# A two layer gated cross attention kernel: layer 0 without mask rows, queries in three transfers, gelu in four parts, value projections at 7, 8 and 10, first loads in order of need on two queues

## What is computed

```python
def _L0_xattn_ref(query, key, value, Wq, bq, Wk, bk, Wv, bv, Wo, bo):   # query is _layernorm(x)
    q = split_heads(query @ Wq.T + bq)
    k = split_heads(key @ Wk.T + bk)
    v = split_heads(value @ Wv.T + bv)
    scores = jnp.einsum('bhqd,bhkd->bhqk', q, k) / np.sqrt(HEAD_DIM)
    weights = jax.nn.softmax(scores, axis=-1)
    out = jnp.einsum('bhqk,bhkd->bhqd', weights, v)
    return out.transpose(0, 2, 1, 3).reshape(b, -1, D_MODEL) @ Wo.T + bo
# layer 1: the same, with scores = jnp.where(m == 0, -1e9, scores) before the softmax
# layer 0's experts: D 128, F 512; layer 1's: D 128, H 64, and a shared one
h = jax.nn.gelu(jnp.einsum('td,edf->etf', xf, w1) + b1[:, None, :], approximate=False)
y = jnp.einsum('etf,efd->etd', h, w2) + b2[:, None, :]
```

## Time and profile before

| | us |
|---|---|
| median of 3 runs | 1044.85 (1041.06 to 1046.26) |
| the profiled execution | 1040.23 |
| its span, first to last instruction | 1038.1 |
| PE busy | 922.5 (89%) |
| DVE busy | 723.0 (70%) |
| ACT busy | 586.2 (56%) |
| POOL busy | 525.0 (51%) |

### The profile page before, as it was taken

How to read it: one execution, slowest core, us unless ns; L and a number is a source line. 1 busy time by engine, 2 the same in 40 slices (tenths; PEclk the granted TensorE clock), 3 DMA queues, 4 the chain that set the end, 5 groups by cost and what they waited for, 6 DMA issues and landing times.

```text
span 1038.1 us, 32346 instructions
## 1 busy us (share of the span) xinstructions
PE 922.5 (89%) x13088; PEld 675.9 (65%) x13088; DVE 723.0 (70%) x1531; ACT 586.2 (56%) x1060; POOL 525.0 (51%) x667
## 2 busy tenths in 40 slices
PE   2487899999999999999999999999999999999974
PEld 0154577777777777777777777666666666666753
DVE  3376576785767768586785867878787878787722
ACT  1044556556565565656547565665757575757560
POOL 5353445543546335453446565665657576672202
PEclk9998899999999999999999999999999999999995
DMA  8735653333323333233465646767676767665200
GB/s 181 133 90 137 145 126 72 72 83 69 63 55 85 70 77 76 37 81 70 95 137 88 143 110 132 162 123 156 124 152 122 145 130 146 137 137 97 52 2 18
DMA packets 95215, 107.24 MB, mean 103 GB/s; under 512 B 22394, under 2 KB 86972, under 8 KB 95068
## 3 DMA queue, kind: packets, MB, share of 16 engines
q1 hardware_dynamic: 95068, 105.19, 49.0%
HBM read 35.89 MB, written 0.46 MB: 35 GB/s over the span
## 4 chain that ended last, share of the span: by engine, by line
PE 66%; DVE 16%; ACT 9%; issue 5%; SPq 2%; DMA 1%; POOL 0%; POOLq 0%; ACTq 0%; DVEq 0%
PE pO L993 13%; PE pMX L1010 12%; PE pST L972 12%; PE pKV L1124 6%; PE pFY L1082 6%; PE pKV L1115 5%; PE pFH L1150 5%; DVE mx L925 4%; DVE mx L920 4%; ACT P L678 3%; DVE rden L839 3%; PE pFY L1047 2%; ACT HR L715 1%; PE pFY L1086 1%; ACT V L696 1%
## 5 line engine op out<-in xcount | busy, mean ns | idle before, releaser
L678 ACT ACTIVATE P<-pST 125x448 f32<-125x448 f32 x768 | 396.1, 542 | 349.9 <-PE pST L972 344.3
L925 DVE TENSOR_REDUCE mx<-pMX 112x1 f32<-112x500 f32 x384 | 258.4, 673 | 172.3 <-PE pMX L1010 172.1
L1010 PE MATMUL pMX<-kop,qmax 104*112 104x500 f16 x768 | 293.1, 392 | 44.7 <-DMA qmax<-qlo 18.5
L972 PE MATMUL pST<-qexp,kop 106*128 106x112 f16 (+1 forms) x3072 | 280.2, 214 | 19.9 <-ACT P L678 9.3
L972 PEld LDWEIGHTS pST<-qexp,kop 106*128 106x128 f16 (+1 forms) x3072 | 209.9, 102 | 127.1 <-issue 42.9
L920 DVE TENSOR_REDUCE mx<-pMX 112x1 f32<-112x500 f32 x384 | 255.8, 666 | 42.8 <-PE pMX L1010 41.9
L993 PE MATMUL pO<-P,V 125*17 125x112 f32 x6144 | 186.0, 262 | 0.0
L993 PEld LDWEIGHTS pO<-P,V 125*17 125x17 f32 x6144 | 136.8, 98 | 46.2 <-issue 36.3
L1010 PEld LDWEIGHTS pMX<-kop,qmax 104*112 104x112 f16 x768 | 99.0, 132 | 93.1 <-issue 21.7
L563 POOL CAST khi<-kfull 128x500 f16<-128x500 f32 x96 | 57.7, 601 | 193.0 <-ACT kfull L691 192.8
L565 POOL TENSOR_TENSOR klo<-kfull,khi 128x500 f16<-128x500 f32 x96 | 109.0, 1135 | 7.8
(11 more groups left out here) (144 smaller groups left out, 1089.6 us busy)
## 6 DMA issues: line engine op xcount, KB each, us to landing
C<-in_ctxT SPq DMA_DIRECT2D x32, 750.0 KB, 6.2
kop<-khi SPq DMA_DIRECT2D x192, 125.0 KB
kop<-maskop SPq DMA_DIRECT2D x48, 437.5 KB
kop<-klo SPq DMA_DIRECT2D x96, 125.0 KB
qexp<-qmax SPq DMA_DIRECT2D x32, 182.0 KB
maskin<-in_mask SPq DMA_DIRECT2D x8, 656.2 KB, 6.2
kop<-maskop SPq DMA_DIRECT2D x2, 1312.5 KB
qmax<-qhi SPq DMA_DIRECT2D x128, 7.0 KB
```

The source lines that it names most:

```text
L678: nc.scalar.activation(P[0:KP, slot, h * 4 * T:(h + 1) * 4 * T], pST[0:KP, h, 0:4 * T], ACT.Exp, scale=EXP_SCALE).then_inc(exp_done, 1)
L925: nc.vector.tensor_reduce(mx[:, s % 2, m // PAIRS, m % PAIRS:m % PAIRS + 1], pMX[0:T, 1, 0:CW], AX.X, ALU.max).then_inc(max_done, 1)
L972: mm = nc.tensor.matmul(pST[0:cols, h, i * T:(i + 1) * T], kop[0:ROWS, b, p, tile * KP:tile * KP + cols], qexp[0:ROWS, b, p, :, :].rearran ...
L1010: nc.tensor.matmul(pMX[0:T, m % 2, 0:CW], qmax[0:SHIFT0, st.s % 2, p, :, :].rearrange("r j q -> r (j q)"), kop[0:SHIFT0, st.s % 2, p, c * ...
```

## The change

- In layer 0 kop, qmax and qexp use 48 rows of keys or queries (`SHIFT0_L0`) and the two shift rows behind them (`ROWS_L0` = 50); no mask and pick rows. The two batches that open layer 1 get shift rows and pick rows by extra transfers. pick is now a 56 x 56 tile, repeated by the transfer.
- DVE writes the queries block-diagonally (head 0 of a pair with zeros beside it, head 1 likewise), multiplied by a column `head_of`; qmax is filled by three transfers per batch instead of six, and no longer cleared at the start.
- The largest scores in ct are laid out by halves of the pairs, and go to qexp in two transfers instead of one.
- Gelu of layer 0 is taken in four parts instead of two, two experts each; gelu stands at kt 9 instead of 8. `experts_of` lets y0 read the first part and y1 the second.
- In even steps with experts (`has_f`) the value projections stand at 7, 8, 10 instead of 8, 9, 10, and at kt 10 PE runs maxima, weighted sums and the projection ahead of the experts and both score halves behind them; ACT copies the values of kt 10 before the exponentials there.
- The first loads come in pieces in the order of need (weights of the keys, x of the first two batches, C in three chunks, the rest); the low halves of the first context and the weights are made by DVE in between. ACT's queue takes the biases, the queries of batch 0, the shift rows and the output weights.

The diff, cut to its core:

```diff
-        uses += [(8, "v0", 1), (9, "v1", 1), (10, "v2", 1)]
+        first = 7 if has_f(s) else 8
+        uses += [(first, "v0", 1), (first + 1, "v1", 1), (10, "v2", 1)]
...
-        uses += [(4, "qT", 2), (5 if s < 0 else 6, "q", 1)]
+        uses += [(2, "qT", 2), (3, "q", 2)] if s < 0 else [(4, "qT", 2), (6, "q", 2)]
...
+        pick = sb("pick", [S, S], F16)
+        shift_rows = sb("shift_rows", [2, SHW], F16)
...
+        def queries(eng, n):
+
+            for row, part in ((0, qhi), (PR, qhi), (2 * PR, qlo)):
+                eng.dma_start(qmax[row:row + PR, n % 2, :, :, :], part[:, n % 2, :, :]).then_inc(qmax_in, 16)
+            if opens_layer(n):
+                eng.dma_start(qmax[MASK0:SHIFT0, n % 2, :, :, :].rearrange("s p j q -> s (p j) q"),
+                              pick[:, :].unsqueeze(1).broadcast_to([S, H, S])).then_inc(qmax_in, 16)
...
-            sp.dma_start(W[:, :], wpack).then_inc(w_in, 16)
-            sp.dma_start(bq_row[:, :], bqrow).then_inc(w_in, 16)
-            sp.dma_start(bc[:, :], bcast.partition_broadcast(128)).then_inc(w_in, 16)
-            sp.dma_start(C[:, :], ctxT[0]).then_inc(c_in, 16)
-            sp.dma_start(X[:, :].rearrange("t (g d) -> t g d", g=G),
-                         x.rearrange("(g t) d -> t g d", g=G)).then_inc(x_in, 16)
-            sp.wait_ge(init_v, 1)
-            sp.wait_ge(init_p, 5)
-            for b in range(2):
-                sp.dma_start(kop[MASK0:SHIFT0, b, :, :],
-                             maskop[0:S, :].unsqueeze(1).broadcast_to([S, PAIRS, S2])).then_inc(init_dma, 16)
-                for i in range(2):
-                    sp.dma_start(kop[SHIFT0 + i:SHIFT0 + i + 1, b, :, :],
-                                 shift_rows[:, i:i + 1, :].broadcast_to([1, PAIRS, S2])).then_inc(init_dma, 16)
-                sp.dma_start(qmax[MASK0:SHIFT0, b, :, :, :],
-                             pick[:, :, :].rearrange("s (p j) q -> s p j q", j=2)).then_inc(init_dma, 16)
+            sp.dma_start(W[:, 0:D], wpack[:, 0:D]).then_inc(wk_in, 16)
+            sp.dma_start(xg(0), x[0:T, :]).then_inc(x0_in, 16)
+            for c in range(CH):
+                sp.dma_start(C[:, c * CW:(c + 1) * CW], ctxT[0, :, c * CW:(c + 1) * CW]).then_inc(c0_in[c], 16)
+            sp.dma_start(W[:, D:], wpack[:, D:]).then_inc(w_in, 16)
+            sp.dma_start(X[:, D:].rearrange("t (g d) -> t g d", g=G - 1),
+                         x[T:, :].rearrange("(g t) d -> t g d", g=G - 1)).then_inc(x_in, 16)
+            sp.dma_start(bc[:, :], bcast.partition_broadcast(128)).then_inc(bc_in, 16)
...
+                if opens_layer(n) and c == CH - 1:
+                    sp.dma_start(kop[SHIFT0:ROWS, dst, :, :].rearrange("r p (i n) -> r (p i) n", n=SHW),
+                                 shift_rows[:, :].unsqueeze(1).broadcast_to([2, PAIRS * S2 // SHW, SHW])
+                                 ).then_inc(kop_in[c], 16)
...
-                    sp.dma_start(qexp[SHIFT0:ROWS, (s - 1) % 2, :, :, :].rearrange("r p j q -> r (p j q)"),
-                                 ct[:, :]).then_inc(shift_in, 16)
+                    for h in range(2):
+                        row = SHIFT0_L0 if layer_of(s - 1) == 0 else SHIFT0
+                        to = qexp[row:row + 2, (s - 1) % 2, HP * h:HP * (h + 1), :, :]
+                        sp.dma_start(to.rearrange("r p j q -> r (p j q)"), ct[PAIRS * h:PAIRS * (h + 1), :]
+                                     ).then_inc(shift_in, 16)
...
+            def early_loads(s, kt):
+
+                if s == -1 and kt == 5:
+                    act.wait_ge(fh_free, upto(fh_uses, s, "q", True))
+                    queries(act, 0)
+                if s == 0 and kt == 0:
+                    act.wait_ge(init_p, 2)
+                    for b in range(2):
+                        act.dma_start(kop[SHIFT0_L0:ROWS_L0, b, :, :].rearrange("r p (i n) -> r (p i) n", n=SHW),
+                                      shift_rows[:, :].unsqueeze(1).broadcast_to([2, PAIRS * S2 // SHW, SHW])
+                                      ).then_inc(init_dma, 16)
+                if s == 0 and kt == 11:
+                    act.wait_ge(init_w, 4)
+                    for g in range(4):
+                        rows = slice(32 * g, 32 * g + PR)
+                        act.dma_start(woE[rows, :, :, :], wo.rearrange("l (r g i) n -> g i l r n", r=2, g=4)[g]
+                                      ).then_inc(wo_in, 16)
+                        act.dma_start(bvE[rows, :, :], bvc.rearrange("l g i r -> g i l r")[g]).then_inc(wo_in, 16)
+                    act.wait_ge(bc_in, 16)
+                    nc.scalar.activation(gains[:, :], bc[:, GX:GX + 4], ACT.Tanh).then_inc(init_a, 1)
...
+                for kt in range(KT):
+                    if has_f(s) and kt == 10:
+                        evacuate(kt)
...
-                    if kt == 8 and has_f(s):
+                    if kt == 9 and has_f(s):
                         act.wait_ge(fh_free, st.at(lambda s: before(fh_uses, s + 1, True)))
                         if layer_of(s - 3) == 0:
-                            for half in (HR[:, 0:E0 * F0C // 2, :], HR[:, E0 * F0C // 2:, :]):
-                                nc.scalar.activation(half, half, ACT.Gelu).then_inc(gelu_done, 1)
+                            for part in range(4):
+                                two = HR[:, 2 * F0C * part:2 * F0C * (part + 1), :]
+                                nc.scalar.activation(two, two, ACT.Gelu).then_inc(gelu_done, 1)
...
-                        link(nc.vector.tensor_copy(qhi[:, :], pFH[:, 0:T]))
-                        nc.vector.tensor_tensor(qlo[:, :], pFH[:, 0:T], qhi[:, :], ALU.subtract).then_inc(fh_free, 1)
+                            dve.wait_ge(qmax_in, q_total(s))
+                        if s == -1:
+                            dve.wait_ge(init_h, 7)
+                        q = pFH[:, 0:T].rearrange("p (b q) -> p b q", b=2)
+                        own = head_of[:, layer_of(s + 1), :]
+                        for j in range(2):
+                            link(nc.vector.tensor_scalar(qhi[:, :, j, :], q, own[:, j:j + 1], None, ALU.mult))
+                        for j in range(2):
+                            nc.vector.scalar_tensor_tensor(out=qlo[:, :, j, :], in0=q, scalar=own[:, j:j + 1],
+                                                           in1=qhi[:, :, j, :], op0=ALU.mult, op1=ALU.subtract
+                                                           ).then_inc(fh_free, 1)
...
+                    if s == -1 and kt == 1:
+                        low_context(0)
+                        query_weights()
+                        low_context(1)
+                    if s == -1 and kt == 2:
+                        low_context(2)
+                    if s == -1 and kt == 5:
+                        other_weights()
...
+                rows, slot = slice(0, SHIFT0_L0 if layer_of(n) == 0 else SHIFT0), i
+                nc.tensor.matmul(pMX[0:T, m % 2, 0:CW], qmax[rows, b, slot, :, :].rearrange("r j q -> r (j q)"),
+                                 kop[rows, b, slot, c * CW:(c + 1) * CW], start=True, stop=True).then_inc(mx_ready, 1)
...
+                    m0 = MAXES_PER_KT * kt
+                    apart_ = has_m(s)
                     late = kt in (1, 7)
-                    if has_m(s) and not late:
-                        max_scores(st, MAXES_PER_KT * kt)
-                    weigh(st, kt)
                     experts = [u[1] for u in fy_uses(s) if u[0] == kt and early(u[1])]
                     if experts:
+                        if has_m(s):
+                            max_scores(st, m0)
+                        weigh(st, kt)
+                        project(kt)
+                        if has_m(s):
+                            max_scores(st, m0 + 1)
                         small("y0")
-                        if has_m(s):
-                            max_scores(st, MAXES_PER_KT * kt + 1)
                         small("y1")
-                    score_half(st, kt, 0)
-                    if has_m(s) and late:
-                        max_scores(st, MAXES_PER_KT * kt)
...
-                    if has_m(s) and not experts:
-                        max_scores(st, MAXES_PER_KT * kt + 1)
-                    score_half(st, kt, 1)
+                        score_half(st, kt, 0)
+                        score_half(st, kt, 1)
```

More of the change, by code:

```diff
@@ L210, in pool_links, with opens_layer, b_total, q_total @@
     return n
[L213 to L215 removed]
+def opens_layer(n):
+    return n in (B, B + 1)
+def b_total(n, c):
+    return sum(48 if layer_of(t) == 0 else 80 if opens_layer(t) and c == CH - 1 else 64 for t in range(n + 1))
+def q_total(n):
+    return sum(48 if layer_of(t) == 0 else 64 if opens_layer(t) else 48 for t in range(n + 1))
+def qexp_total(n):
+    return 16 * (n // 2 + 1)
 class Step:
@@ L502, in step @@
                         apart(sp)
-                        sp.wait_ge(qexp_in[(s - 1) % 2], st.at(lambda s: 16 * ((s - 1) // 2 + 1)))
```

(8 more changed lines are left out.)

310 lines of the change are left out of this document (181 added, 129 removed).

## The result

The changed kernel takes 1078.49 us (median of 4 runs, 1075.65 to 1087.02) against 1045.22 for the kernel before: a ratio of 1.0335, 95% interval 1.0294 to 1.0376. It is 3.35% slower, where 1031.6 was forecast. The profiled execution has a span of 1077.8 us against 1038.1, so 39.7 us have to be found.

What follows compares the result with a forecast made beforehand. PE was taken as nearly full in the steps and nearly idle in a 38 us start. Terms -18.1 + 2 + 4.9 - 2 = -13.2, from the median 1044.85, gave 1031.6 us, range 1021 to 1040.

Steps and rivals of the forecast that it cites:

- No mask rows in layer 0: Layer 0's matmuls: time goes by columns, so fewer rows give PE 0; extra transfers opening layer 1 at most 3 us once.
- Rival 3: After the start: PE's clock stays low, running 18 us longer at half pace and losing 9 us: 1040.6; chance 8%.
- The start: First loads and queries: first maxima start at 20.0 instead of 38.11 us, -18.1 us.
- the forecast's far end: In the start: first maxima at 24.7 if queries land 5.2 us after the last issue's start and C's issue stalls.
- the rule on shared engines: In the start: transfers from different issuers share 16 DMA engines, so first maxima come up to 2.4 us after 20.0.
- The queries: Odd steps, DVE: four instructions instead of two, 0.22 us a step in layer 0, 0.42 in layer 1: +4.9 us.
- Gelu and value projections: Even steps: reordered work ends them 0.1 us earlier in layer 0, 0.15 in layer 1: -2 us (-20 to +10).
- The shift rows: Two transfers instead of one, second issue 0.6 us later where PE already waits: +2 us (0 to 5).
- Rival 1: Even steps around kt 9: the reorder removes most waits on ACT, up to -20 us instead of -2: 1023; chance 12%.
- rival 2: The start is cut less: first maxima at 24.7 instead of 20.0 us, total 1036; chance 18%.
- Rival 4: Even steps: PE stands through a table load and the four quarters' extra 0.4 us, +27 us: 1061; chance 4%.

Runs made afterwards that it cites:

- undivided: The changed kernel, with layer 0's matmuls on 48 and 50 rows issued with PE's array undivided: 1045.33 us (ratio 1.0030).
- the runs on 106, 66 and 50 rows: Changed kernel's early start, array undivided, old queries from batch 2 on, layer 0's maxima and scores on these rows: 1029.79, 1036.31, 1048.44 us.
- the zeros on 66 rows: An earlier run: the changed kernel, layer 0's maxima and scores on 66 rows, 16 of them zeros written by transfers: 1046.43 us (ratio 1.0013).
- the old queries: Changed kernel with undivided array, queries from batch 2 on made by two instructions and six transfers as in the kernel before: 1045.60 us (ratio 1.0007).
- the run that was to tell them apart: The changed kernel with the array undivided for batches 0 and 1 only, default division from batch 2 on: 1078.48 us (ratio 1.0312).

## Why the prediction was wrong

**The step that failed** is "No mask rows in layer 0": *A matmul's time goes by its columns ... so fewer rows give PE* 0. Its rows compare 104 rows with 128 and were stretched to 48, beyond the border. In its place the runs showed a price of 0.09 us for each change between the divided and the undivided array: steps 5 to 16 take 410.26 us in the changed kernel and 381.93 undivided, and by the ratios (1.0335 and 1.0030) the division costs some 32 of the 46.9 us between forecast and measurement. The rest is of the size of what few rows cost by the pace, the second thing that the term left out (18.7 us between 106 rows and 50). The trace of the kernel before had nearer rows for the first price: layer 1's experts have 64 rows there. A timeline of PE there (expert on 64 rows, maximum), then one in layer 0 (expert on 128 rows, maximum):

```profile
674.80 0.66 PE L1086 MATMUL pFY<-w2b,HR 64*112 64x128 f32 x4
675.39 0.42 PE L1010 MATMUL pMX<-kop,qmax 104*112 104x500 f16 x1
```

```profile
489.01 1.97 PE L1082 MATMUL pFY<-w2a,HR 128*112 128x128 f32 x16 [1.17 <-ACT HR L715]
490.82 0.38 PE L1010 MATMUL pMX<-kop,qmax 104*112 104x500 f16 x1
```

Behind 64 rows the maximum starts 0.07 before the group's end, behind 128 rows 0.16 before; from the start of the group's last matmul to that of the maximum the medians are 199 and 109 ns. 19 changes a step at these 0.09 would have been 27 us in 16 steps. The Trainium skill (TensorEngine Tiling (Array Packing), section Tiling Modes) says that a change of tiling mode drains TensorE. The traces agree that a change costs time and give the price, 93 ns into a block and 91 out of it; that it is a drain, they do not show. The prediction did not weigh that rule against this edit.

**Rival 3, the low pace**, had the right sign and the wrong cause: the pace rose 83 us after the first maxima instead of 18.4, and the runs on 106, 66 and 50 rows, with the same early start, tie that to the rows. It was priced at 9; steps 1 and 2 lost 16.8, the divisions in them included. One wait illustrates it: PE waits 3.46 in the kernel before and 3.35 in the undivided run for the shift rows of step 3; the low stretch behind it lasts 5.0 us there and 19.7 here.

```profile
122.57 0.53 PE L972 MATMUL pST<-qexp,kop 106*128 106x112 f16 x4 [3.46 <-issue]
```

```profile
114.19 0.53 PE L433 MATMUL pST<-qexp,kop 50*128 50x112 f16 x4 [3.35 <-issue]
```

**The start** was right in what releases it: the queries land at 19.96 (forecast 20.0). That the time agrees to 0.04 is luck. The last query transfer is issued at 14.67 and not at 17.2, and it needs 5.3 us to land and not 2.8; the forecast's far end had 5.2 for the landing, from the kernel before. A longer landing fits the rule on shared engines that the prediction cites, and so do the 4.3 us behind the zeros on 66 rows; which transfers the queries shared with here was not tested.

```profile
14.67 0.62 ACTq L440 DMA_DIRECT2D qmax<-qlo  x1
```

Of the 18.1 only 14.9 arrive at the first ct, mainly because step 0 then runs wholly at the lower pace (from the first maxima to ct PE is busy for 23.1 us, before 19.9; the divisions are in it). In the run on 106 rows 14.5 arrive there (46.08), and its profile ends 13.1 us before that of the kernel before.

**The queries** were priced at +4.9: measured 0.42 in an odd step of layer 0 and 0.31 in layer 1 (0.22 and 0.42 forecast); 7 and 8 steps at that are 5.4. **Gelu and value projections**, -2: even steps are 0.10 shorter in layer 0 and 0.29 in layer 1 (0.1 and 0.15 forecast), and the waits before the experts and at kt 11 are 0.71 and 0.44 undivided, 0.58 and 0.34 in the changed kernel (0.85 and 0.5 forecast). **The shift rows**, +2: not separated; the 0.20 by which odd steps of layer 1 remain longer with the old queries (28.42 against 28.22) bounds it. **Rival 1** did not occur. Of **rival 2** the longer landing did, and the earlier issue made up for it. **Rival 4** had the direction, slower, and not the cause: even steps grew by 1.9 us, but PE's waits for ACT in them became shorter. Even without the two effects of rows the sum of the prediction does not quite stand: for the run on 106 rows, with the old queries, it would be -18.1 (the 4.9 left out), and 13.7 were measured (1029.79 against 1043.51 for the kernel before beside it), most of the difference from the start, 14.5 instead of 18.1.

What is left open: whether the two shares of steps 1 and 2 in the changed kernel, pace and division, add up as in the separate runs (the run that was to tell them apart missed); why the pace goes by rows; and what lets the length of a low stretch differ between executions of one kernel.

## What to carry to other kernels

Before rows are cut from a matmul, look at who stands beside it: here a block of 64 rows or fewer among blocks of more paid at both borders; rows of zeros (66 rows) avoided that, and an undivided tile did too. Where a kernel's first steps run at the lower clock, try full rows there: the undivided 50 rows lost 18.7 us against 106 rows of mostly zeros. The rows were cut in all of layer 0, so whether full rows in the first steps alone would do was not tested. And bound a price by a row of the trace that has the new size, even if it belongs to another part of the program.

## What the runs showed of the hardware

- The cost of a change of division is hidden in the busy time: PE read 32.62 of 33.30 us busy, and only spacings of starts (50 to 141 ns, 112 to 205) gave it away.
- The granted clock can stay at 0.50 for 20.00 us in which PE is busy for 20.00 (undivided run, 66.60 to 86.60, where some 66 of 190 matmuls are on 48 and 50 rows). The same rows do not bring it down later: in that run it reads 1.00 all through steps 5 to 18.
- The Trainium skill (TensorE: Matmul & The Clock Gate, section Part 1: The HAM clock gate) makes the clock depend on how busy PE has been. The traces agree only in part: after 11.6 us busy in the same 16 us, PE reached the higher level at 38.2, 45.0 and 71.6 us on 106, 66 and 50 rows. So the number of rows counts too, zero rows included.
- Two profiles of the kernel before repeat its three low stretches within 0.1 us of length, but the kernel on 66 rows spread over 14.7 us. Low stretches of two kernels are to be compared over several executions of each.
